# Self-attention run batch by batch, its projections kept in SBUF and moved there by direct transfers, with the head of the kernel and the loops written out

## The chip, the cores and the metric

The kernel runs on one core of one Trainium2 chip. The metric is the device time of one execution in microseconds (us), lower being better. The core has a matrix engine (TensorE, PE in the rows), a vector engine (VectorE, DVE), an activation engine (ScalarE, ACT), a general engine (GpSimd, POOL) and a queue engine that issues most of the transfers (SyncE, SP). Each engine works through its own instructions in order and waits on semaphores for the others.

## The reference, cut to what matters

One decoder layer on 2 batches of 1024 tokens with 256 features: layer norm, causal self-attention with 16 heads of 16 features, an 8-step recurrent state update, a feed-forward block, cross-attention to 77 context tokens, and a block of decision trees. The change touches the first two only:

```
x = x + attn_block(_layernorm(x))            # in it a second norm, _ln(x, g_attn, b_attn), comes first:
xn = _ln(x, g_attn, b_attn)
qkv = (xn @ qkv_w + qkv_b).reshape(b, s, 3, H, HD)       # H = 16 heads of HD = 16
scores = jnp.einsum('bhqd,bhkd->bhqk', q, k) / np.sqrt(HD)
scores = jnp.where(causal[None, None], -jnp.inf, scores)
attn_w = jax.nn.softmax(scores, axis=-1)
attn = jnp.einsum('bhqk,bhkd->bhqd', attn_w, v)
attn = attn @ out_w + out_b
x = x + attn
```

## The kernel before, in words

Everything is held transposed: 128 partitions carry features, the free axis carries tokens. The 2048 tokens are four **chunks** of 512; chunks 0 and 1 are batch 0, chunks 2 and 3 are batch 1. The queries and keys make four projection **tiles** of 128 features for each chunk (two of queries, two of keys), so there are 16 tiles. A tile is a float32 product in two matmuls (`qk_projection`, L1623). The values are another 8 groups of projections (L1636).

Self-attention works on **quads**: four heads of one batch. There are 8 quads. For each quad two things are computed.

1. The **maxima**. 36 **units** (L1664) multiply 128 queries by 128 keys of four heads, each into one PSUM bank of a ring of three (banks 5 to 7), with a second, masking matmul (L1667) on the 8 diagonal ones. VectorE reduces each unit (`maximum`, L1208), then reduces the 8 partial maxima (`gather`, L1219); TensorE transposes the result (`turn`, L1684); VectorE negates it (`negate`, L1226), and a transfer writes it as two extra rows of the queries (`load_max`, L560).
2. The **scores**, in 12 steps (L1692), with keys in the partitions. Queries and keys are split in a high and a low part, stacked as 3 x 16 rows a head, so that a fast one-pass matmul gives nearly float32 precision. ScalarE takes the exponential (L878), GpSimd masks the diagonal blocks (L737), TensorE multiplies by the values with a column of ones for the sums (`weigh`, L1710), ScalarE copies the result out (`read_out`, L890).

TensorE's order is written by hand: during quad n it runs the scores and `weigh` of n, and between them the units of quads n+1 and n+2 (`ahead`, by a list `plan` that shares 36 units over the 12 steps). Before quad 0 it must run all 36 units of quad 0 and the first 8 of quad 1.

All re-arranging goes through DRAM. The high and low parts (`part_hi`, `part_lo`) of each tile are stored three times (`store_parts`, L467), 12 transfers of 256 KB a chunk, and loaded again for each quad: q1 and k1 for the units (`load_first`, L533, L538), q2 and k2 for the scores (`load_second`, L548, L552). Results are stored (L473) and loaded back (`pack`, L483, L491), the sums inverted on VectorE (L1236), stored and spread over partitions (`spread`, L499, L503). The quads go tile by tile: both batches of the first tile, then both of the second. The four tiles of batch 1 for each of its two chunks are projected beside the units of quad 0 (`qk_beside`). The engines run quads 2 to 5 in a hardware loop of two turns (`over_iterations`); the others are written out.

At the head, GpSimd presets k1, k2, q1, q2 and vq; two of its instructions at L693 write rows of ones. VectorE, ScalarE and TensorE do the norms of four chunks in a fixed skew of five stages (`skewed`), and the projections start after chunk 3.

## Time and profile before

| | us |
|---|---|
| median of 3 runs | 1054.2 (1047.81 to 1059.79) |
| the profiled execution, its own time | 1045.27 |
| its span, first to last instruction | 1043.5 |
| TensorE busy in the span | 917.5 (88%) |
| VectorE busy | 597.1 (57%) |
| ScalarE busy | 472.9 (45%) |
| GpSimd busy | 178.5 (17%) |
| mean granted TensorE clock | 0.915 of 2.4 GHz |

The profiled execution lies 8.9 us below the median of the three runs and just under the fastest of them. Shares of the whole span are means over stages with different limits, so they say little on a stage. The self-attention ends at about 382 us; the rest of the layer follows and is not changed.

### The profile page before, as it was taken

How to read it: one execution, taken by the hardware profiler on the slowest of the kernel's cores; microseconds unless marked ns; L12 is line 12 of the kernel's file. 1: busy time of each engine (PE TensorE's matmuls, PEld its weight loads, DVE VectorE, ACT ScalarE, POOL GpSimd, SP SyncE). 2: the span in 40 equal slices, each digit the busy share in tenths (PEclk: the TensorE clock that was granted, in tenths of full speed). 3: DMA queues.
4: the chain of work that ended last, by engine and by line, in shares of the span. 5: the costliest groups of instructions: out<-in, count | busy, mean ns of one | idle time of the engine just before them, and what ended most of it. 6: DMA issues, size and time to landing. Idle time of an engine off the chain costs nothing. (4 is left out here: it accounts for less than half of the span.)

```text
span 1043.5 us, 11787 instructions
## 1 busy us (share of the span) xinstructions
PE 917.5 (88%) x3897; PEld 557.2 (53%) x3912; DVE 597.1 (57%) x898; ACT 472.9 (45%) x681; POOL 178.5 (17%) x206
## 2 busy tenths in 40 slices
PE   5776689999999986999997899988887898899997
PEld 3553345554555433544444777754333666667775
DVE  4635767777777415377786664453434555546554
ACT  2311055565665662466654455524534323434332
POOL 7920012211122211000002340000015700000000
PEclk9797789999999997899998999996657999899999
DMA  3056534323443115100000000122745200000000
GB/s 124 9 201 171 216 101 112 101 61 95 104 112 101 37 60 192 48 0 1 0 1 7 12 1 1 36 56 43 139 98 131 79 1 20 1 1 21 1 21 20
DMA packets 27953, 66.15 MB, mean 63 GB/s; under 512 B 6048, under 2 KB 8992, under 8 KB 27520
## 3 DMA queue, kind: packets, MB, share of 16 engines
q1 hardware_dynamic: 24896, 62.00, 21.2%
q0 software_dynamic: 1472, 2.37, 1.1%
q10 hardware_dynamic: 1536, 1.14, 0.4%
q8 instruction: 29, 0.48, 0.2%
q14 instruction: 20, 0.16, 0.1%
HBM read 37.09 MB, written 19.14 MB: 54 GB/s over the span
## 5 line engine op out<-in xcount | busy, mean ns | idle before, releaser
L1208 DVE TENSOR_REDUCE part_max<-psum 128x4 f32<-128x512 f32 x288 | 186.0, 687 | 78.2 <-PE psum L1664 46.4
L878 ACT ACTIVATE prob<-psum 128x1024 f32<-128x1024 f32 (+1 forms) x192 | 145.4, 809 | 92.8 <-PE psum L1692 92.1
L1664 PE MATMUL psum<-k,q 128*128 128x512 f32 x288 | 121.8, 468 | 22.4 <-DMA k<-k 16.5
L1692 PE MATMUL psum<-q,k 128*128 128x512 f32 (+3 forms) x384 | 96.9, 358 | 11.0 <-ACTq L865 9.9
L1664 PEld LDWEIGHTS psum<-k,q 128*128 128x128 f32 x288 | 52.7, 196 | 85.9 <-DVE part_max L1208 55.4
L1061 ACT ACTIVATE silu<-psum,wt_bias 128x512 f32<-128x512 f32 x64 | 40.6, 686 | 116.5 <-PE psum L350 108.6
L737 POOL TENSOR_SCALAR_AFFINE_SELECT prob<-prob 128x256 f32<-128x256 f32 x128 | 52.1, 416 | 240.0 <-ACT prob L878 239.0
L1710 PE MATMUL psum<-prob,vq 128*32 128x512 f32 (+3 forms) x768 | 81.8, 498 | 2.4 <-POOL prob L737 1.6
L1692 PEld LDWEIGHTS psum<-q,k 128*128 128x128 f32 x384 | 66.2, 191 | 32.2 <-issue 11.2
L1540 DVE TENSOR_TENSOR masked_lo<-masked,masked_hi 128x1024 fp32r<-128x1024 f32 x32 | 41.2, 1288 | 40.7 <-ACT masked_hi L1068 40.7
L348 PE MATMUL psum<-masked_hi,wt_hi 128*128 128x512 f32 x128 | 56.3, 440 | 3.6 <-DVE masked_lo L1540 3.6
L348 PE MATMUL psum<-tree_hi,wt_hi 128*128 128x512 f32 x128 | 56.5, 442 | 1.6 <-ACT silu L1061 1.6
L1529 DVE TENSOR_SCALAR decide<-psum,wt_bias 128x512 bf16<-128x512 f32 x32 | 24.0, 751 | 56.9 <-PE psum L350 56.9
L1861 PE MATMUL psum<-act_u,early 128*128 128x512 f32 x128 | 55.8, 592 | 0.0
L1861 PE MATMUL psum<-nrm,early 128*128 128x512 f32 x128 | 55.6, 592 | 0.0
L349 PE MATMUL psum<-nrm_lo,wt_hi 128*128 128x512 f32 x128 | 53.2, 415 | 0.0
L350 PE MATMUL psum<-tree_hi,wt_lo 128*128 128x512 f32 x128 | 52.5, 410 | 0.0
L1611 PE MATMUL psum<-ident,rs 128*128 128x128 f32 x192 | 36.0, 354 | 16.8 <-DVE rs L1120 10.3
L1388 DVE TENSOR_REDUCE xrow_max<-psum 128x4 f32<-128x312 f32 x64 | 29.5, 480 | 36.6 <-PE psum L1807 36.3
L350 PE MATMUL psum<-masked_hi,wt_lo 128*128 128x512 f32 x128 | 50.1, 392 | 0.0
L349 PE MATMUL psum<-masked_lo,wt_hi 128*128 128x512 f32 x128 | 49.9, 390 | 0.0
L1611 PEld LDWEIGHTS psum<-ident,rs 128*128 128x128 f32 x192 | 33.7, 260 | 24.5 <-DVE rs L1120 15.0
(156 smaller groups left out, 1632.8 us busy)
## 6 DMA issues: line engine op xcount, KB each, us to landing
q<-q SPq DMA_DIRECT2D x8, 768.0 KB, 6.5
k<-k SPq DMA_DIRECT2D x16, 384.0 KB, 8.2
xq<-xq_b SPq DMA_DIRECT2D x36, 128.0 KB
q<-part_hi SPq DMA_DIRECT2D x16, 256.0 KB
k<-part_hi SPq DMA_DIRECT2D x16, 256.0 KB
o<-stage SPq DMA_DIRECT2D x8, 512.0 KB, 7.0
wt<-in_wt SPq DMA_DIRECT2D x8, 512.0 KB, 4.3
nrm<-in_xT SPq DMA_DIRECT2D x4, 512.0 KB, 5.8
```

The costliest lines, as they stand in the source:

```text
L348: pe.matmul(out, rounded(w_hi), rounded(x_hi), start=start, stop=False)
L349: pe.matmul(out, rounded(w_hi), rounded(x_lo), start=False, stop=False)
L350: return pe.matmul(out, rounded(w_lo), rounded(x_hi), start=False, stop=stop)
L737: pool.affine_select(out=blk, in_=blk, compare_op=ALU.is_ge, fill=0.0, base=0, pattern=[[0, 2], [1, P]], channel_multiplier=-1)\
L878: act.activation(A.prob[0:A.keys, s % 2, p, :, q0:CH], psum[0:A.keys, 2 * p:2 * p + 2, q0:CH], ACT.Exp, scale=SCALE)\
L1208: dve.tensor_reduce(part_max[:].rearrange("q (j p i) k -> q p j i k", j=2, p=2)[:, :, :, i, kt], heads, AX_X, ALU.max).then_inc(A.s1_free, 1)
L1540: dve.tensor_tensor(rounded(masked_lo[:, st.buf]), masked[:, st.buf], masked_hi[:, st.buf], ALU.subtract)\
L1611: mm = pe.matmul(bank((L.bank(c), 4)[i])[:, t * P:(t + 1) * P], rs[:, c % 2, i, t:t + 1].to_broadcast([P, P]), ident[:], start=True, stop= ...
L1664: mm = pe.matmul(heads, A.q1[:, qd, i * P:(i + 1) * P], A.k1[:, qd, :, k0:k0 + P], start=True, stop=not diag)
L1692: mm = pe.matmul(psum[0:A.keys, 2 * p + j, q0:CH], A.k2[:, qd, p, j, kt * P:kt * P + A.keys], A.q2[:, qd, p, c * CH + q0:(c + 1) * CH], st ...
L1710: mm = pe.matmul(psum[32 * h:32 * h + 32, 4, q0:CH], A.vq[:, qd, kt, h, :], A.prob[:, s % 2, h // 2, h % 2, q0:CH], start=first, stop=last)
L1861: mm = pe.matmul(bank(2 * c + m), wx01[:, k, m * P:(m + 1) * P], state(n)[:, k, cols_of(c)], start=False, stop=k == 1, skip_group_check=True)
```

## The change

- The products of the query and key projections stay in SBUF, in `nat_hi` (rounded) and `nat_lo`: ScalarE writes each tile twice (`qk_high`), and GpSimd subtracts (`qk_low`), where VectorE did it before. There are no DRAM copies q3, k3, o3.
- The units take `nat_hi` itself as queries, in its natural layout of 8 heads in 128 rows, against k1 that is zero outside the quad's 64 rows. q1 is gone. k1, q2 and k2 are filled by transfers inside SBUF: 4 for k1, 18 for q2 and k2 of a quad (6 of 32 rows and 12 of 16 rows), where 5 and 3 did it from DRAM. The results go from `stage` to their places by 5 such transfers in place of 1 store and 1 or 2 loads.
- The quads go batch by batch. Only batch 0's 8 tiles are projected at the head; the 8 tiles of batch 1 are projected inside quads 1 and 3, one in each of their score steps 4 to 7, each in a bank of the ring of three.
- The head is written out by hand in a new order: projections of chunk 0 begin while the norms of chunks 2 and 3 are still under way, and the units of quad 0 stand between the norms. The values are projected after that, between the last units of quad 0, and ScalarE copies them out; GpSimd adds the bias when it packs them for a quad (`copy_values`).
- GpSimd's presets start without waiting for the constants; the two instructions at L693 are replaced by two transfers; presets of q1 and sums are gone.
- All quads are written out; the hardware loop is gone. The shares of `plan` are rounded another way (steps 3 and 5 have 1 and 4 units in place of 2 and 3).
- The second norm has a scratch of its own, since the spread sums now lie in `wide`.

```diff
-            def store_qk(batch):
-                for c in by_batch[batch]:
-                    for m in range(4):
-                        sp.wait_ge(qk_free, 4 * c + m + 1 + 3)
-                        store_parts(sp, q3 if m < 2 else k3, part_hi, part_lo, m, c % 2, ...)
+            def load_k1(n, done, at):
+                b, m, qd = place(n)
+                if n >= 2:
+                    sp.wait_ge(mx_turned, n - 1)
+                for h in range(4):
+                    rows = slice(64 * qd + HD * h, 64 * qd + HD * h + HD)
+                    sp.dma_start(k1[rows, qd, h, at].bitcast(F32), nat_hi[rows, 2 + m, at]).then_inc(done, 16)
+            def load_q2k2(n):
+                b, m, qd = place(n)
+                if n >= 2:
+                    sp.wait_ge(st_ps, 2 * SSTEPS * (n - 1))
+                for r in range(3):
+                    for p in range(2):
+                        rows = slice(64 * qd + 32 * p, 64 * qd + 32 * p + 32)
+                        sp.dma_start(q2[32 * r:32 * r + 32, qd, p, :].bitcast(F32), ...)
+                        for j in range(2):
+                            sp.dma_start(k2[32 * r + HD * j:32 * r + HD * j + HD, qd, p, j, :].bitcast(F32), ...)
+            for n in range(XQUADS):
+                if n + 2 < XQUADS:
+                    load_k1(n + 2, k1_in[qd], whole)
+                if 2 <= n + 1 < XQUADS:
+                    load_q2k2(n + 1)
+                if n >= 1:
+                    pack_self(n - 1)
+                if n >= 2 and n % 2 == 0:
+                    spread_self(n // 2 - 1)
+                if n + 1 < XQUADS:
+                    load_neg_max(n + 1)
...
+        QK_TILES = [(c, t) for c in range(2) for t in (2, 0, 3, 1)] \
+            + [(c, t) for m in range(KT) for c in (2, 3) for t in (2 + m, m)]
+        def qk_tile_of(n, step):
+            return QK_TILES[8 + 2 * (n - 1) + step - 4] if n in (1, 3) and 4 <= step < 8 else None
...
+            def qk_low(c, t):
+                pool.wait_ge(qk_raw, qk_at(c, t) + 1)
+                pool.tensor_tensor(nat_lo[:, t, at].bitcast(F32R), nat_lo[:, t, at], nat_hi[:, t, at], ALU.subtract)
...
+            def qk_high(c, t):
+                act.wait_ge(qk_ps, qk_at(c, t) + 1)
+                act.activation(nat_hi[:, t, at].bitcast(F32R), qk_bank(c, t), ACT.Identity, bias=v_("bqk", t))
+                act.activation(nat_lo[:, t, at].bitcast(F32), qk_bank(c, t), ACT.Identity, bias=v_("bqk", t))
...
+            for n in range(XQUADS):
+                pe.wait_ge(q2k2_in[qd], 16 * 18 * (n // 2 + 1))
+                pe.wait_ge(neg_in[qd], 16 * (n // 2 + 1))
+                for s in range(SSTEPS):
+                    scores(n, s, 0)
+                    ahead(n, s, 0)
+                    scores(n, s, 1)
+                    ahead(n, s, 1)
+                    if qk_tile_of(n, s):
+                        qk_projection(*qk_tile_of(n, s))
+                    if s > 0:
+                        weigh(n, s - 1)
```

On TensorE at the head, before the change, all norms come first (mean L1590, variance L1598, spreading L1611), then 8 tiles of batch 0 (L1623), then all values (L1636), then the units:

```order
6 L1611 MATMUL psum<-ident,rs 128x128 x8
7 L1598 MATMUL psum<-mean_w,wide 128x1 x4
8 L1611 MATMUL psum<-ident,rs 128x128 x8
9 L1598 MATMUL psum<-mean_w,wide 128x1 x4
10 L1611 MATMUL psum<-ident,rs 128x128 x16
11 L1623 MATMUL psum<-nrm,w 128x512 x16
12 L1636 MATMUL psum<-w,nrm 128x256 x32
13 L1664 MATMUL psum<-k,q 128x512
```

After the change the same place on TensorE (spreading L1542, tiles L1558, variance L1529, mean L1521, units L1592):

```order
3 L1542 MATMUL psum<-ident,rs 128x128 x8
4 L1521 MATMUL psum<-wide,mean_w 128x512
5 L1542 MATMUL psum<-ident,rs 128x128 x8
6 L1558 MATMUL psum<-nrm,w 128x512 x4
7 L1529 MATMUL psum<-mean_w,wide 128x1 x4
8 L1558 MATMUL psum<-nrm,w 128x512 x2
9 L1521 MATMUL psum<-wide,mean_w 128x512
10 L1558 MATMUL psum<-nrm,w 128x512 x4
11 L1592 MATMUL psum<-k,nat_hi 128x512
12 L1595 MATMUL psum<-causal_b,ident_b 128x512
13 L1592 MATMUL psum<-k,nat_hi 128x512
14 L1558 MATMUL psum<-nrm,w 128x512 x2
```

The first tiles stand ahead of the norms of chunks 2 and 3, and the values (L1570, not in these rows) have moved behind the fifteenth unit and later.

On TensorE in quad 1, from the third score step of its second half on, before the change (scores L1692, weigh L1710):

```order
147 L1692 MATMUL psum<-q,k 128x512 x2
148 L1664 MATMUL psum<-k,q 128x512
149 L1692 MATMUL psum<-q,k 128x512 x2
150 L1664 MATMUL psum<-k,q 128x512
151 L1667 MATMUL psum<-causal_b,ident_b 128x512
152 L1710 MATMUL psum<-prob,vq 32x512 x4
153 L1664 MATMUL psum<-k,q 128x512 x2
```

After it, at the same place (scores L1614, weigh L1631):

```order
157 L1614 MATMUL psum<-q,k 128x512 x2
158 L1592 MATMUL psum<-k,nat_hi 128x512
159 L1614 MATMUL psum<-q,k 128x512 x2
160 L1592 MATMUL psum<-k,nat_hi 128x512
161 L1595 MATMUL psum<-causal_b,ident_b 128x512
162 L1558 MATMUL psum<-nrm,w 128x512 x2
163 L1631 MATMUL psum<-prob,vq 32x512 x4
164 L1592 MATMUL psum<-k,nat_hi 128x512 x2
```

A tile of two matmuls has come in ahead of `weigh`; four such places are in quad 1 and four in quad 3.

On SyncE, one turn of the steady order before the change, of quad 1 (L560 is the write of the maxima):

```order
51 L533 DMA q<-q 64x1x1024
52 L538 DMA k<-k 16x1024 x4
53 L548 DMA q<-q 96x2x1024
54 L552 DMA k<-k 48x2x1024 x2
55 L473 DMA o<-stage 128x1024
56 L483 DMA nrm<-o 64x1x1024
57 L560 DMA q<-neg_max 2x16x128
```

After it, the last part of the turn of quad 2 (k2 and q2 loads L486 and L482, sums L500, results L502, inverse sums L508 and L511, maxima L493):

```order
58 L482 DMA q<-nat_hi 32x1024
59 L486 DMA k<-nat_hi 16x1024 x2
60 L482 DMA q<-nat_lo 32x1024
61 L486 DMA k<-nat_hi 16x1024 x2
62 L500 DMA sums<-stage 64x1x64
63 L502 DMA nrm<-stage 16x1024 x4
64 L508 DMA r<-recip 128x64
65 L511 DMA wide<-r 128x1x1024
66 L493 DMA q<-neg_max 2x16x128
```

The write of the maxima, the last row of each, now stands behind 4 + 18 + 5 transfers of its turn, and 2 more in every second turn, in place of 10 to 12.

## Rows read from the trace of the kernel before

**Rows 1.** Windows of the first stage: us, busy of each engine, granted clock.
```profile
20.00:40.00 20.00, 13.83 (x66) 12.44 (x66) 14.81 (x26) 6.00 (x12) 19.74 (x4) 0.74 0.00 0
60.00:80.00 20.00, 11.59 (x54) 9.87 (x52) 5.66 (x16) 0.00 (x0) 1.16 (x2) 0.86 0.53 204
80.00:100.00 20.00, 11.86 (x33) 6.30 (x34) 9.45 (x16) 2.07 (x3) 0.00 (x0) 0.71 0.70 166
120.00:140.00 20.00, 9.98 (x31) 5.97 (x30) 7.92 (x13) 4.57 (x5) 1.08 (x3) 0.60 0.50 171
160.00:200.00 40.00, 38.59 (x239) 20.64 (x238) 29.12 (x47) 22.39 (x32) 9.27 (x23) 1.00 0.33 87
```

**Rows 2.** Timeline of TensorE at the head: start, duration, what, idle before.
```profile
21.70 2.66 PE L1611 MATMUL psum<-ident,rs 128*128 128x128 f32 x16
...
43.77 14.02 PE L1623 MATMUL psum<-nrm,w 128*128 128x512 f32 x32
57.62 13.98 PE L1636 MATMUL psum<-w,nrm 128*128 128x256 f32 x64
88.14 0.77 PE L1664 MATMUL psum<-k,q 128*128 128x512 f32 x1 [16.55 <-DMA k<-k]
...
118.86 0.39 PE L1684 MATMUL psum<-ident,row_max 128*32 128x128 f32 x1 [1.24 <-DVE row_max L1219]
...
133.88 1.19 PE L1692 MATMUL psum<-q,k 128*128 128x512 f32 x2 [9.92 <-ACTq L865]
```

**Rows 3.** Timeline of ScalarE at the head: the first bias, the first exponential.
```profile
26.50 1.38 ACT L848 ACTIVATE nrm<-nrm,vec 128x512 f32<-128x512 f32 x2
...
134.00 1.28 ACT L878 ACT_TABLE_LOAD   x1 [21.80 <-DMA k<-part_hi]
```

**Rows 4.** Timeline of TensorE in quad 6, one score step and the next.
```profile
342.34 0.63 PE L1692 MATMUL psum<-q,k 128*128 128x512 f32 x2
342.81 0.39 PE L1664 MATMUL psum<-k,q 128*128 128x512 f32 x1
343.03 0.63 PE L1692 MATMUL psum<-q,k 128*128 128x512 f32 x2
...
344.05 1.06 PE L1710 MATMUL psum<-prob,vq 128*32 128x512 f32 x8
...
345.62 0.62 PE L1692 MATMUL psum<-q,k 128*128 128x512 f32 x2
```

**Rows 5.** Timeline of ScalarE: the third step of quads 1, 2, 4 and 5.
```profile
173.66 1.08 ACT L878 ACTIVATE prob<-psum 128x512 f32<-128x512 f32 x2 [1.44 <-PE psum L1692]
...
205.49 1.08 ACT L878 ACTIVATE prob<-psum 128x512 f32<-128x512 f32 x2 [1.33 <-PE psum L1692]
...
268.95 1.08 ACT L878 ACTIVATE prob<-psum 128x512 f32<-128x512 f32 x2 [1.33 <-PE psum L1692]
...
301.98 1.08 ACT L878 ACTIVATE prob<-psum 128x512 f32<-128x512 f32 x2 [1.32 <-PE psum L1692]
```

**Rows 6.** Lines by source: duration min/median/max in ns, where they lie.
```profile
L467 SPq DMA_DIRECT2D q<-part_hi x16: 657/1196/1472, 48.9 to 115.6; - x16
L642 SPq DMA_DIRECT2D quot_b<-stage x32: 508/589/610, 713.2 to 802.4; - x32
L1208 DVE TENSOR_REDUCE part_max<-psum x288: 629/692/695, 89.5 to 350.5; 128x4 f32<-128x512 f32 x144
L766 POOL TENSOR_TENSOR res<-res,x x8: 1267/1634/1728, 549.4 to 594.5; 128x512 f32<-128x512 f32 x8
L1147 DVE TENSOR_TENSOR rs<-rs x4: 161/163/3264, 15.8 to 34.0; 128x4 f32<-128x4 f32 x4
L693 POOL TENSOR_SCALAR k<-k,ident x2: 10617/10624/10632, 28.3 to 39.1; 2x4096 fp32r<-2x4096 f32 x2
```

**Rows 7.** Timeline of SyncE and VectorE after the last quad.
```profile
382.49 0.33 SPq L473 DMA_DIRECT2D o<-stage  x1
385.18 0.58 SPq L483 DMA_DIRECT2D nrm<-o  x1
...
390.99 0.55 DVE L1236 RECIPROCAL recip<-sums 128x64 f32<-128x64 f32 x1 [12.61 <-DMA sums<-o]
...
400.00 1.23 DVE L1282 TENSOR_TENSOR nrm<-nrm,den 128x1024 f32<-128x1024 f32 x1 [6.66 <-DMA den<-r]
```

More of the change, by code:

```diff
@@ L43 @@
 SCALE = HD ** -0.5
-R2 = 3 * HD
+LEAD = 8
 LOW = -1e30
@@ new lines, in layer @@
+        self_units = [(kt, i) for i in range(SEQ // P) for kt in range(i + 1)]
+        SUNITS = len(self_units)
+        self_todo = [(1, u) for u in range(LEAD, SUNITS)] + [(2, u) for u in range(LEAD)]
+        self_plan = [[] for _ in self_steps]
+        for _at, _unit in enumerate(self_todo):
+            done = [CH - st[2] + 64 for st in self_steps]
+            step = next(i for i in range(SSTEPS) if (_at + 0.5) * sum(done) <= SUNITS * sum(done[:i + 1]))
+            self_plan[step].append(_unit)
@@ L712, in _ @@
             pool.tensor_copy(causal_b[:], caus_f[:])
[L713 to L732 removed]
+            pool.memset(vq[:], 1.0).then_inc(zeros_set, 1)
@@ new lines, in _, with read_out @@
+            first_bias(3)
+            for u in range(8):
+                keep_values(u)
+            def read_out(n, c):
+                b, m, qd = place(n)
+                act.wait_ge(pv_ps, 2 * n + c + 1)
+                if n >= 2 and c == 0:
+                    last = n - 2
+                    act.wait_ge(num_in[last // 4][qd], 16 * 4 * (last // 2 % 2 + 1))
+                    act.wait_ge(sum_in[qd], 16 * (n // 2))
+                act.activation(stage[:, qd, c * CH:(c + 1) * CH], bank(4), ACT.Copy).then_inc(o_done, 1)
@@ new lines, in turn, with scores @@
+            def turn(n):
+                pe.wait_ge(mx_row, n + 1)
+                pe.wait_ge(*slot_free(turn_slot[n]))
+                pe.transpose(bank(5 + turn_slot[n] % 3, P)[0:32], row_max[:], ident[:]).then_inc(mx_turned, 1)
+            def scores(n, s, p):
+                b, m, qd = place(n)
+                c, kt, q0, diag, first, last = self_steps[s]
+                g = n * SSTEPS + s
+                if g > 0:
+                    pe.wait_ge(prob_ready, 2 * g + p - 1)
+                for j in range(2):
+                    mm = pe.matmul(bank(2 * p + j)[:, q0:CH], k2[:, qd, p, j, kt * P:(kt + 1) * P],
+                                   q2[:, qd, p, c * CH + q0:(c + 1) * CH], start=True, stop=True)
+                mm.then_inc(st_ps, 1)
@@ new lines, in weigh @@
+            def weigh(n, s):
+                b, m, qd = place(n)
+                c, kt, q0, diag, first, last = self_steps[s]
+                g = n * SSTEPS + s
+                if s == 0:
+                    pe.wait_ge(vq_ready, n + 1)
+                if first:
+                    pe.wait_ge(o_done, 2 * n + c)
+                if diag:
+                    pe.wait_ge(prob_masked, 2 * (n * DIAGS + sum(st[3] for st in self_steps[:s + 1])))
+                pe.wait_ge(prob_ready, 2 * g + 2)
+                for h in range(4):
+                    mm = pe.matmul(psum[32 * h:32 * h + 32, 4, q0:CH], vq[:, qd, kt, h, :],
+                                   prob[:, s % 2, h // 2, h % 2, q0:CH], start=first, stop=last)
+                if last:
+                    mm.then_inc(pv_ps, 1)
@@ new lines, in ahead @@
+            def ahead(n, s, quarter):
+                for at, u in share(n, s, quarter):
+                    unit(at, u)
+                if turns_after(n, s, quarter):
+                    turn(n + 1)
+            mean(ln1)(0)
+            mean(ln1)(1)
+            variance(ln1)(0)
+            variance(ln1)(1)
+            spread_out(ln1)(0)
+            mean(ln1)(2)
+            spread_out(ln1)(1)
+            qk_projection(0, 2)
+            qk_projection(0, 0)
+            variance(ln1)(2)
@@ new lines, in _ @@
+            qk_projection(0, 3)
+            mean(ln1)(3)
+            qk_projection(0, 1)
+            qk_projection(1, 2)
+            unit(0, 0)
+            unit(0, 1)
+            qk_projection(1, 0)
+            spread_out(ln1)(2)
+            variance(ln1)(3)
+            for u in range(2, 6):
+                unit(0, u)
+            qk_projection(1, 3)
+            qk_projection(1, 1)
+            for u in range(6, SUNITS):
+                unit(0, u)
+                if u == 9:
+                    spread_out(ln1)(3)
+                if u % 3 == 2 and u // 3 in range(4, 12):
+                    values_of(u // 3 - 4)
```

821 lines of the change are left out of this document (333 added, 488 removed).

## The prediction

> **What bounds the kernel now.** I read the windows by stage first, then the timelines of the head, then one quad step by step. The self-attention has three parts with three limits.
>
> The *head*, until the first scores at 133.88 us [rows 2], is bound by SyncE's queue. TensorE does its 8 tiles and the values by 71.6 us and then stands idle 16.55 us for k1, does the units, and stands idle 9.92 us more ahead of the first scores; ScalarE's wait there ends with a store of a key tile, 21.80 us [rows 3]. The stores are 48 transfers of 256 KB at a median of 1.196 us [rows 6], 57 us of queue between 48.9 and 122 us. In the windows TensorE is busy about half of the time there, and its granted clock is 0.60 to 0.86 [rows 1].
>
> The *quads* are bound by TensorE: 38.59 us busy of 40, clock 1.00, VectorE 29, ScalarE 22 [rows 1]. A step in which all parts are whole lasts 3.28 us from scores to scores (342.34 to 345.62), and TensorE is fed through all of it: 0.22 us from unit to next scores (342.81 to 343.03), and 1.06 for weigh [rows 4]. A quad takes 31.8 us (173.66 to 205.49) [rows 5].
>
> The *end* is a chain of transfers: last result stored at 382.49, loads from 385.18, inverse at 390.99, product at 400.00 [rows 7].
>
> **The change, part by part.**
>
> *Head: the removed waits.* All stores and the DRAM loads go. What is late next is TensorE itself, since its hand-written list now holds everything. In the trace the first bias of chunk 0 begins at 26.50 [rows 3]; its spreading (21.70, 2.66 us) now stands right after the variance of chunk 1, about 2 us earlier. But the spreading of chunk 1 stands ahead of the first tile, so I put that tile at 27.5. From there to the transpose of the maxima TensorE has 8 tiles, 14.0 us, and the values, 14.0 us [rows 2]; 36 units and 8 masks at 0.22, 9.7 us [rows 4]; and the rest of the norms of chunks 2 and 3, for which I take 12 us, from 13.83 busy in the window from 20 to 40 us that holds nearly all of that work [rows 1]. That is 49.7 us. For waits in order (variance of chunk 2, the first units, VectorE's norm work between maxima) I add 7 us. The transpose is then at 84.2. Before, 15.0 us passed from the transpose (118.86) to the scores (133.88), because the queue was full [rows 2]; now a gather and a negation (under 1 us in all), an issue of 0.6 and a landing stand there, 5 us. Scores begin at 89 to 90; I take 89.5. VectorE is no later: 36 maxima at 0.69, 25 us [rows 6], and some 15 us of norms after about 36 us end near 76. So the head gives 133.9 - 89.5 = 44.4 us. Bounds: without the 7 us of waits and with a chain of 4 us it is 52; with a quarter of the 49.7 us at half the clock, as the windows of the old head have it, it is 44.4 - 12.4 = 32.
>
> SyncE in the new head: 12 transfers for k1, then 18 for q2 and k2, at 0.59 us each as small transfers inside SBUF take [rows 6]: 18 us between about 30 and 60 us, under TensorE's work. The 18 for quad 1 stand behind the wait for the maxima of quad 0, go out from 86 to 97 us, and are wanted at 121. GpSimd's 8 subtractions at 1.6 us [rows 6] are done well before the values. The two instructions at L693, 10.6 us each, go; they were hidden, except as follows.
>
> *A rule on the shared port.* One VectorE instruction, L1147, took 3264 ns in place of 163, at 34.00 us, and it lies within L693 on GpSimd [rows 6]. The Trainium skill ("SBUF — State Buffer", Who interferes with whom) says that a VectorE instruction with two SBUF inputs waits for a GpSimd instruction that reads SBUF. That rule speaks against the change, which gives GpSimd 16 subtractions and 8 sums with SBUF inputs; by it the three additions of chunks 2 and 3 at the head could each wait up to 1.6 us, 5 us, against 3.1 us that go with L693. It would move the sum by under 2 us, since VectorE is not last there, and the maxima read PSUM.
>
> *Tiles in the quads.* 8 tiles now stand in steps 4 to 7 of quads 1 and 3, where TensorE has no free time [rows 4]. Before, they lay at the head among the units, under VectorE and the queue. Each costs 1.75 us [rows 2]: 14 us. From below: part of a step is waiting on VectorE's banks, so 1.0 us each, 8 us. From above: a tile takes a bank of the ring of three until ScalarE has read it twice (2 x 0.69, by the 1.38 of a bias pair [rows 3]); the unit three places later waits for that, but a weigh, two units and two scores, some 2.0 us, stand between, so I take nothing for it, and 1.25 us each as an upper bound, 24 us in all. ScalarE has room: 1.94 + 1.38 us in a step that grows to about 5.
>
> *Transfers in a quad.* 28 issues in a turn, 30 in every second one, at 0.59 us: 17 us of 31.8. The maxima's rows come last in it, but their value is ready only about 27 us into the quad, so nothing waits, with 8 us to spare. The price is that of stage to quot_b in the cross-attention, the same form [rows 6].
>
> *Written-out loops, new shares.* The quad outside the loop lasted 31.83 us (1 to 2), the pair across the middle 31.8 each, and only quad 4 to 5 lasted 33.03 [rows 5], where VectorE waited for the sums to land. I take 1 us for that and nothing for the loop. The Trainium skill ("Runtime: NRT & Kernel Launch", Instruction fetch mechanics) says that a taken branch makes a fetch stall. By it, unrolling would gain something at each turn; the rows of quads inside and outside agree to 0.1 us, so the sum has nothing of it.
>
> *End.* One store and one load become one transfer: 385.18 - 382.49 = 2.7 us, and the sums no longer stand behind the result's load (0.6) [rows 7]. The last chunks' product comes 4 us earlier; bounds 0 and 6.5. The order by batch changes nothing here: batch 0 was ready ahead of the end before, too.
>
> *Sum.* Span 1043.5 - 44.4 + 14 - 1 - 4 = 1008.1; with the 1.8 us that lie around it 1009.9. The median of three runs is 8.9 us above the profiled execution, whose time agrees with the lowest run within 2.5. I take half of that distance: **1014 us**, 3.8% below the median before.
>
> **The rivals.**
>
> 1. *The head runs cold.* TensorE waits in small pieces between norms, tiles and units, the granted clock stays between 0.5 and 1, and scores begin at 102. For: the old head had 0.60 to 0.86 [rows 1]. Against: the clock was 1.00 wherever tiles followed each other (14.02 us for 8). Time 1014 + 12.4 = 1026. Chance 0.13.
>
> 2. *The ring costs more than the tile.* Each tile costs 3.0 us for the bank and for exponentials behind two more copies on ScalarE. 8 x 1.25 = 10: 1024. Chance 0.10.
>
> 3. *Better than that.* Tiles half hidden (-6) and a head nearer its bound (-4 to -8): 1000 to 1004. Chance 0.12.
>
> 4. *SyncE's queue becomes the bound of every quad, and the kernel is slower.* If each issue takes as long as the stores at the head did, the 18 loads and 5 results stand between the start of a quad and the write of the maxima. A turn is then 24 issues plus a landing of 2.4 us, and 26 plus about 8 in turns with the inverse sums. Over six turns: 150 p + 31 - 191 us of delay. At 1.2 us it is 20 us, 1034. The whole gain of 35.4 is gone at p = 1.3 us; at the 1.472 of the longest q store [rows 6] it is 61 us, 1014 + 61 = 1075. Against: those were 256 KB each, these are 64 or 128 KB and the same form took 0.508 to 0.610. Chance 0.05, all slower.
>
> 5. *The change does not shorten the head.* The chain by chunks orders TensorE so badly that scores start near 124, 10 us before the old start, which the tiles eat: 1048, no change. Chance 0.04.
>
> The forecast itself, 1003 to 1024, has 0.56.
>
> **How the numbers follow.** The range must leave out no more than 0.2. It takes in cases 1 and 2 and most of 3, and the mild form of 4 (1034): 996 to 1036. A change under 1% (10 us) is about what a measurement of this kernel can't tell from none, as its three runs span 12 us. Faster by over 1%, under 1044: cases 0 to 3, 0.91. Same: most of case 5, 0.04. Slower: case 4, 0.05.
>
> **What would show it.** First exponential near 90 us (134 before). 8 tiles at the head and four in each of quads 1 and 3; those quads 38 to 39 us from third step to third step, the others 31.8. No TensorE wait on q2, k2 or the maxima's rows ahead of a quad; issues on SyncE near 0.6 us. GpSimd's subtractions near 1.6 us. Last weigh near 350, product of chunk 2 some 14 us later in place of 19. From there on the timeline is the old one, shifted by 35 us. I am wrong if the head's units wait one by one, if a quad's start waits for a transfer, or if the steps with tiles last over 6 us.

## The result and the profile after

The changed kernel takes 1004.8 us (median of 4 runs, 1001.6 to 1007.0); the kernel before, run beside it, 1051.0 us. The ratio is 0.9589 with the interval 0.9553 to 0.9625: 4.1% faster, 46.2 us. The profiled execution after has 1004.79 us and a span of 1002.8, so the two profiled spans differ by 40.7 us.

Windows of the first stage, which answer to [rows 1]:

```profile
20.00:40.00 20.00, 18.38 (x70) 11.35 (x69) 11.73 (x22) 9.31 (x17) 10.27 (x7) 1.00 0.04 8
40.00:60.00 20.00, 14.74 (x69) 9.06 (x67) 14.52 (x26) 8.56 (x16) 7.96 (x6) 0.97 0.50 93
60.00:80.00 20.00, 19.66 (x77) 16.07 (x78) 13.26 (x22) 3.94 (x7) 0.00 (x0) 0.85 0.05 8
```

TensorE (the first number) is busy 18.4, 14.7 and 19.7 of 20 us where it had been half idle, at a granted clock of 1.00, 0.97 and 0.85. The last mean hides a cold stretch: TensorE waited 2.76 us for VectorE's maxima ahead of a unit at 60.34, and from 60 to 64 us the granted clock was 0.50; it was back at 1.00 by 68.

Timeline of TensorE at the head, which answers to [rows 2]: the first tile, the end of the maxima of quad 0, the first scores.

```profile
27.03 2.05 PE L1542 MATMUL psum<-ident,rs 128*128 128x128 f32 x16 [1.62 <-DVE rs L1116]
28.91 1.45 PE L1558 MATMUL psum<-nrm,w 128*128 128x512 f32 x3
...
83.38 0.27 PE L1604 MATMUL psum<-ident,row_max 128*32 128x128 f32 x1
...
84.42 0.47 PE L1592 MATMUL psum<-k,nat_hi 128*128 128x512 f32 x1 [0.53 <-DVE part_max L1134]
...
87.50 0.62 PE L1614 MATMUL psum<-q,k 128*128 128x512 f32 x2
```

The first scores come at 87.50 in place of 133.88. Timeline of ScalarE, which answers to [rows 3] and [rows 5]: the table load and first exponential, the third steps of quads 0 to 2.

```profile
83.73 1.28 ACT L853 ACT_TABLE_LOAD   x1
88.16 1.94 ACT L853 ACTIVATE prob<-psum 128x1024 f32<-128x1024 f32 x2 [3.15 <-PE psum L1614]
...
93.17 1.09 ACT L853 ACTIVATE prob<-psum 128x512 f32<-128x512 f32 x2 [1.22 <-PE psum L1614]
...
124.04 0.60 ACT L853 ACTIVATE prob<-psum 128x512 f32<-128x512 f32 x1 [1.20 <-PE psum L1614]
...
162.75 0.60 ACT L853 ACTIVATE prob<-psum 128x512 f32<-128x512 f32 x1 [1.20 <-PE psum L1614]
```

The first exponential was at 135.30 and is at 88.16: 47.1 us earlier. From third step to third step a plain quad takes 30.87 us (31.8 before), a quad with four tiles 38.71.

TensorE's timeline in the step with the transpose of the maxima (transpose, scores, next unit), in quad 2, first in the kernel before, then in the changed one:

```profile
223.90 0.27 PE L1684 MATMUL psum<-ident,row_max 128*32 128x128 f32 x1
223.93 0.94 PE L1692 MATMUL psum<-q,k 128*128 128x384 f32 x4
225.40 0.50 PE L1664 MATMUL psum<-k,q 128*128 128x512 f32 x1 [0.53 <-DVE neg_max L1226]
```

```profile
181.16 0.27 PE L1604 MATMUL psum<-ident,row_max 128*32 128x128 f32 x1
181.19 0.94 PE L1614 MATMUL psum<-q,k 128*128 128x384 f32 x4
181.97 0.47 PE L1592 MATMUL psum<-k,nat_hi 128*128 128x512 f32 x1
```

Before, the transpose went into bank 7, which the units use too, and the third unit of the quad whose maxima come next waited until VectorE had read and negated it (`pe.wait_ge(A.neg, n + 1)` in `unit`). After the change the transpose takes the next bank of the ring in turn, and that wait is gone: the unit behind the scores goes out 0.7 us sooner. In the rows the wait shows only as the 0.53 in brackets.

Timeline of SyncE and VectorE after the last quad, which answers to [rows 7]:

```profile
342.68 0.59 SPq L500 DMA_DIRECT2D sums<-stage  x1
343.31 2.40 SPq L502 DMA_DIRECT2D nrm<-stage  x4
345.76 0.58 SPq L508 DMA_DIRECT2D r<-recip  x1
347.75 0.66 SPq L511 DMA_DIRECT2D wide<-r  x1
...
344.69 0.55 DVE L1157 RECIPROCAL recip<-sums 128x64 f32<-128x64 f32 x1 [29.29 <-DMA sums<-stage]
...
354.63 1.23 DVE L1166 TENSOR_TENSOR nrm<-nrm,wide 128x1024 f32<-128x1024 f32 x1 [6.30 <-DMA wide<-r]
```

The last weigh starts at 341.56 (381.31 before), the product 13.1 us behind it (18.7 before).

**Where the 46 us are**, by marks in the two traces: first exponential -47.1; from there to the last weigh 253.4 us in place of 246.0, +7.4; to the product -5.6; to the first SiLU of the trees -0.5 (815.00 and 769.18), in all -45.8. Behind it nothing is changed, but the trees took 233.6 us in place of 228.5. Windows of that stretch, before and after:

```profile
815.00:1043.50 228.50, 206.56 (x851) 155.57 (x866) 120.40 (x121) 80.64 (x106) 16.00 (x9) 0.97 0.04 12
```

```profile
769.20:1002.70 233.50, 212.15 (x866) 159.59 (x866) 120.65 (x121) 80.56 (x106) 16.12 (x9) 0.95 0.04 12
```

This is the same work at a granted clock of 0.95 in place of 0.97. In the profiled runs below, whose trees are unchanged, the stretch took 226.9 to 233.8 us, so this is from run to run. The difference of the medians, 46.2, is close to the 45.8 of the marks ahead of it.

### The profile page after: what moved, and what is told of

Its sections match the earlier page's. It is cut to its first block and busy times, and to the rows that moved or that the text cites. A ratio compares the mean times of both kernels' runs of the same rounds, so it can differ in the third digit from the quotient of the medians.

```text
span 1002.8 us, 11132 instructions
## 1 busy us (share of the span) xinstructions
PE 909.9 (91%) x3912; PEld 554.0 (55%) x3912; DVE 577.7 (58%) x865; ACT 485.7 (48%) x705; POOL 181.7 (18%) x218
## 5 line engine op out<-in xcount | busy, mean ns | idle before, releaser
L1592 PE MATMUL psum<-k,nat_hi 128*128 128x512 f32 x288 | 118.9, 454 | 6.4 <-DVE part_max L1134 5.0
L1614 PE MATMUL psum<-q,k 128*128 128x512 f32 (+3 forms) x384 | 96.7, 354 | 1.4 <-ACT prob L853 1.4
L1592 PEld LDWEIGHTS psum<-k,nat_hi 128*128 128x128 f32 x288 | 51.6, 190 | 66.1 <-issue 52.9
L1631 PE MATMUL psum<-prob,vq 128*32 128x512 f32 (+3 forms) x768 | 81.8, 498 | 1.3 <-POOL prob L677 1.2
L1614 PEld LDWEIGHTS psum<-q,k 128*128 128x128 f32 x384 | 65.1, 189 | 22.5 <-ACT prob L853 11.6
L979 ACT ACTIVATE xprob<-psum 77x1024 f32<-77x1024 f32 x32 | 31.6, 1015 | 28.0 <-PE psum L1770 27.3
L1542 PE MATMUL psum<-ident,rs 128*128 128x128 f32 x192 | 32.6, 329 | 12.5 <-DVE rs L1083 10.4
```

Source lines behind the costliest of these rows:

```text
L1592: mm = pe.matmul(heads, rounded(nat_hi[:, m, i * P:(i + 1) * P]), k1[:, qd, :, kt * P:(kt + 1) * P], start=True, stop=i != kt)
L1614: mm = pe.matmul(bank(2 * p + j)[:, q0:CH], k2[:, qd, p, j, kt * P:(kt + 1) * P], q2[:, qd, p, c * CH + q0:(c + 1) * CH], start=True, stop ...
L1631: mm = pe.matmul(psum[32 * h:32 * h + 32, 4, q0:CH], vq[:, qd, kt, h, :], prob[:, s % 2, h // 2, h % 2, q0:CH], start=first, stop=last)
```

## The experiments

Runs of one kernel differ by 0.5 to 2% in all, mostly behind the attention. In the traces the same quad of the changed kernel repeats within 0.05 us, and the first exponential lay between 87.34 and 88.61 in six profiled runs with the head of the changed kernel, and at 94.24 in a seventh (experiment 10). So small terms are read from marks: the first exponential, the third step of each quad, the last weigh, the product of the third chunk. Times without a range are medians of 2 to 6 runs. Where a cut of an edit leaves lines out, it has `...`.

**1. No tiles in the quads.** `qk_tile_of` gives none, and the projections of batch 1 are left out: batch 1 uses those of batch 0.

```diff
-            return QK_TILES.index((c, t))
+            return QK_TILES.index((c % 2, t))
...
-            return QK_TILES[8 + 2 * (n - 1) + step - 4] if n in (1, 3) and 4 <= step < 8 else None
+            return None
```

> The changed kernel without the 8 projection tiles in quads 1 and 3: batch 1 reuses the projections of batch 0. It leaves out the projections of batch 1. Theory (a tile costs its TensorE time and a little of the ring): the quads with tiles fall from 38.7 to 30.9 us, 8 x 1.96 = 15.7 us less than the changed kernel, near 989 us. By my prediction's price of 1.75 it is 14 us. Rival (part of a tile lies in time in which TensorE waits anyway, and the two long quads are long for another reason): under 10 us, above 995.

Measured: 982.4 us, ratio 0.9409 [0.935, 0.9467]. The third steps of quads 1 to 4 lie at 124.50, 155.38, 186.26 and 217.12: 30.9 us from each to the next, in the quads that had tiles too. To the last of them (307.80 against 323.00, with a start 0.45 us later) 15.65 us are gone, 1.96 for a tile. The first reading holds: a tile costs its TensorE time, 1.75, and on average 0.2 more.

**2. The wait behind the transpose put back.**

```diff
+                if u == 2 and n >= 1:
+                    pe.wait_ge(mx_neg, n)
                 if at >= 3:
                     pe.wait_ge(*slot_free(at))
```

> The changed kernel with one wait of the old one put back: the third unit of the quad after next, behind the transpose of the maxima, waits until VectorE has negated that transpose, as the fixed bank made it do. Nothing is left out. Theory (the bank of the transpose in the ring is what made the plain quads shorter): the step with the transpose grows by 0.7 us, plain quads from 30.9 to 31.6, six or seven times, 4 to 5 us in all, near 1009. Rival (the new shares of units in the steps made them shorter): no change, 1005.

Measured: 1008.0 us. Plain quads go from 30.87 to 31.6 us (quad 2: 163.32 to 194.93), tiled ones from 38.71 to 39.38. From the third step of quad 0 to that of quad 7 it is 234.2 us in place of 229.8, 4.4 us for six transposes. So 0.73 of the 0.95 us by which plain quads became shorter is this wait.

**3. The kernel before with its loop written out.**

```diff
-            with eng.Fori(int(peel_first), ITS - 1) as it:
-                for qd in range(QUADS):
-                    body(it, qd, 2)
+            for it in range(int(peel_first), ITS - 1):
+                for qd in range(QUADS):
+                    body(it, qd, 2)
```

> The kernel before with its loop over the quads written out on every engine; nothing else is changed. Theory: the loops cost nothing, ratio 1.00 within 0.2%, quads at 31.8. Rival (each turn of a loop costs a stall in the fetch of instructions, and this is part of the 0.95 us by which the plain quads are shorter in the changed kernel): quads inside the loop near 31.0, 3 to 5 us less in all, ratio 0.996.

Measured: from third step to third step 31.80 to 31.82 us, no shorter than in the loop (31.70 to 31.82 without the long quad). But the one long quad, 33.03 (268.95 to 301.98 [rows 5]), is gone. VectorE and SyncE there, first in the kernel before, then with the loop written out:

```profile
274.56 0.68 SPq L483 DMA_DIRECT2D nrm<-o  x1
275.51 0.66 SPq L491 DMA_DIRECT2D sums<-o  x1
...
281.34 0.55 DVE L1236 RECIPROCAL recip<-sums 128x64 f32<-128x64 f32 x1 [1.93 <-DMA sums<-o]
```

```profile
273.89 0.58 SPq L483 DMA_DIRECT2D nrm<-o  x1
274.59 0.62 SPq L491 DMA_DIRECT2D sums<-o  x1
...
280.26 0.55 DVE L1236 RECIPROCAL recip<-sums 128x64 f32<-128x64 f32 x1
```

In the loop the sums were issued 6.56 us behind the quad's third step, written out 4.85 us (third step at 269.74), and landed in time: VectorE's 1.93 us of waiting went. The whole kernel did not gain: 1056.4 against 1048.2, ratio 1.011 [1.0057, 1.0163]. Up to the product at 399.85 (400.00) the profiled run, which is the shortest of the six, shows nothing of a loss, and at the first SiLU it is 1.4 us late. Why the timed runs are 8 us longer isn't shown; at least they speak against any gain from written-out loops as such.

**4. The kernel before with a third of the stores.** `q3` and `k3` hold one part; the loads read it three times.

```diff
             for r in range(3):
                 part = part_lo if r == r_lo else part_hi
+                if r != 0:
+                    sp.sem_inc(done, 16)
+                    continue
                 sp.dma_start(out3[:, r, :, at], part[:, half, m_of, :]).then_inc(done, 16)
...
```

> The kernel before with one store of three: of each projection tile only the first of three copies goes to DRAM, and all three parts of the loads read it. It leaves out the low parts of queries and keys, so the scores lack their correction. 16 of 48 stores are left, and 9 more loads stand in each quad. Theory (the old head is bound by the queue of the stores, 1.2 us each): first scores come 25 to 35 us earlier than 133.9, near 100 to 108, and the time falls by about as much; quads stay at 31.8. Rival (the old head is bound by TensorE's order of work, or its cold clock): under 10 us earlier.

Measured: the first exponential at 109.11 in place of 135.30, 26.2 us earlier, quads of 31.8. So over half of the 47.1 us that went from the head was the queue of stores; which part of the other 20.9 us is the loads through DRAM, batch 1's tiles or the order of the work, no run separates. The time is 1034.8, ratio 0.9878 [0.9817, 0.9938], a gain of half of the 26.2. In the profiled run three steps, in quads 2, 4 and 6, took 5.4 to 6.7 us back, 18.6 in all, so that the last weigh is only 9.9 us earlier. Each is of this form on VectorE:

```profile
193.93 0.55 DVE L1242 RECIPROCAL recip<-sums 128x64 f32<-128x64 f32 x1 [5.62 <-DMA sums<-o]
```

My edit had put 9 more loads ahead of the sums, and a wait of VectorE for them stops the maxima and then TensorE. This led to experiment 6.

**5. Half of the values' projection.**

```diff
-                    for k in range(KT):
+                    for k in range(1):
...
```

> The changed kernel with half of the values' projection: each of the 16 products takes one half of the contraction only, which is left out of the result. TensorE has 7 us less to do between the first tile and the transpose of the maxima. Theory (the new head is bound by TensorE's own list): the first exponential comes 5 to 7 us earlier than 88.2. Rival (it is bound by VectorE's maxima and norms, which would leave TensorE waiting in its place): under 2 us earlier.

Measured: first exponential at 83.35, 4.8 us earlier for 7.0 us less of TensorE work (4.0 to 5.3 by the spread of the other heads); quads unchanged; 993.9 us. So TensorE's list sets some two thirds of the 7 us. Behind that VectorE's maxima are last: they run without a break from 73.28 on and end at 78.20, and the transpose waits for their gather and begins at 78.71.

**6. Twice the transfers for the same bytes.** Each of the 18 transfers of a quad's queries and keys is cut in two by columns.

```diff
-                        sp.dma_start(q2[32 * r:32 * r + 32, qd, p, :].bitcast(F32),
-                                     (nat_lo if r == 2 else nat_hi)[rows, m, :]).then_inc(q2k2_in[qd], 16)
+                        for at in (slice(0, CH), slice(CH, SEQ)):
+                            sp.dma_start(q2[32 * r:32 * r + 32, qd, p, at].bitcast(F32),
+                                         (nat_lo if r == 2 else nat_hi)[rows, m, at]).then_inc(q2k2_in[qd], 16)
...
```

> The changed kernel with each of the 18 transfers of queries and keys cut in two, so that the queue of SyncE has 18 more issues in each quad for the same bytes. Nothing is left out. Theory (an issue costs 0.6 us whatever its size, and the slack of the queue is small at one place): the sums of a quad are issued 11 us later, land near 182 in place of 171, and the reciprocal that stands in VectorE's maxima at 173 waits some 9 us, in quads 2, 4 and 6; 20 to 27 us in all, near 1030, while the other quads stay at 30.9 and no quad's start waits. Rival (my rival 4, in which the start of each quad waits for the row of the maxima): 3 to 8 us in every quad, first in quads without a reciprocal too. Third (the queue has room): under 2 us.

Measured: 1031.0 us, ratio 0.9847 [0.9777, 0.9918], 26 us more than the changed kernel by the medians, and 23 without the longest of the four runs (1047.9). By the marks 31.9 us are added up to the last third step: quads 2, 4 and 6 grow by 10.2, 9.6 and 9.4 us, quads 1, 3 and 5 by nothing, and quad 0 by 2.6. Timeline of SyncE and VectorE in quad 2:

```profile
179.61 2.49 SPq L488 DMA_DIRECT2D k<-nat_hi  x4
182.15 0.63 SPq L502 DMA_DIRECT2D sums<-stage  x1
...
184.19 0.55 DVE L1159 RECIPROCAL recip<-sums 128x64 f32<-128x64 f32 x1 [8.26 <-DMA sums<-stage]
```

and of TensorE behind it:

```profile
185.44 0.77 PE L1594 MATMUL psum<-k,nat_hi 128*128 128x512 f32 x1 [7.45 <-DVE part_max L1136]
```

An issue costs the same 0.62 us for half of the bytes. The queue does become the bound, but not as rival 4 had it: no quad's scores waited at their start. The 2.6 us in quad 0 are an idle stretch of TensorE ahead of a unit at 113.59: the loads of k1 for quad 2, the last in that queue, went out from 109.34 to 111.76, and the last of them landed at 113.50. In the changed kernel the sums are issued at 168.99 and the reciprocal comes at 173.11; with the 2 us that such a transfer takes to land (182.15 to 184.19), the slack there is 2 us, some three issues. Of the three reciprocals amid maxima it has the least (in quads 4 and 6 the sums are issued 5.7 and 4.7 us ahead, here 4.1), and the prediction looked at another place.

**7. The end of the last quad through DRAM.**

```diff
+                if n == XQUADS - 1:
+                    sp.dma_start(o3.rearrange("h s d n -> (h s d) n"), stage[:, qd, :]).then_inc(o_st, 16)
+                    sp.wait_ge(o_st, 16)
...
+                    return
...
```

> The changed kernel, in which the result and the sums of the last quad alone go through DRAM as before: one store, a wait, a load of the result and then one of the sums. Nothing is left out. Theory (the end is shorter because one landing and the place behind the result's load are gone): from the last weigh to the product of the third chunk 18 to 19 us in place of 12.7, 5.5 to 6.5 us more. My prediction's price: 4 us more. Rival (it was the order by batch that shortened it): under 1 us.

Measured: last weigh at 341.63, product at 360.40, 18.8 us between them, where the changed kernel has 13.1 and the kernel before 18.7. The whole term is this, 5.7 us. The time is 1008.6 us.

**8. Tiles in short steps.**

```diff
-            return QK_TILES[8 + 2 * (n - 1) + step - 4] if n in (1, 3) and 4 <= step < 8 else None
+            return QK_TILES[8 + 2 * (n - 1) + (2, 3, 10, 11).index(step)] if n in (1, 3) and step in (2, 3, 10, 11) else None
```

> The changed kernel with the four tiles of quads 1 and 3 in steps 2, 3, 10 and 11 instead of 4 to 7. These steps have small scores, and TensorE is not full in them: from the scores of the fourth step to those of the fifth pass 1.70 us, in which its scores, one unit and one weigh take about 0.9. Theory: a tile fills part of that time and costs 1.0 to 1.4 us in place of 1.96, so 4.5 to 7.5 us less than the changed kernel, near 999. Rival (every step is a chain through ScalarE and the ring, and a tile in it adds its whole time and the wait for a bank): 38.7 us for a quad with tiles as before, 1005 or more.

Measured: the tiled quads take 37.76 and 37.78 us in place of 38.71 and 38.68, 1.72 us a tile. Neither reading holds: the short steps have no free TensorE time to give, and what went is only the 0.2 us a tile above its TensorE time. In quad 4 another 1.1 us was lost: ScalarE issues three loads there, and one took 1.93 us in place of 0.86. The median, 998.4, is 6.4 us lower, but the product in the profiled run is only 0.7 us earlier; the rest lies in unchanged work behind.

**9. One small VectorE instruction moved.**

```diff
             dve.wait_ge(c_in, 64)
-            dve.tensor_scalar(b1_scaled[:], vec[:, VEC["b1"][0]:VEC["b1"][0] + KT], 1 / (DT * DT), None, ALU.mult)\
-                .then_inc(b1_set, 1)
...
                 if u == 0:
                     negate(0)
+            dve.tensor_scalar(b1_scaled[:], vec[:, VEC["b1"][0]:VEC["b1"][0] + KT], 1 / (DT * DT), None, ALU.mult)\
+                .then_inc(b1_set, 1)
```

> The changed kernel with one small VectorE instruction, the scaling of b1 (128 x 2), moved from the start to behind the first maxima of quad 1. Nothing is left out. In the changed kernel it takes 1.77 us at 6.22 and ends with GpSimd's first memset of k (1.04 to 7.96), and the squares behind it end at 7.99; before it took 0.17, since that memset began at 7.47 only. Theory (this instruction waits for the memset, and the chain of the first norm behind it): the squares end near 7.0, and everything to the first exponential is 0.5 to 1.3 us earlier, near 87. Rival (it is the memset that slows every VectorE instruction, or the head hides it): the squares still end at 8.0, or the first exponential stays at 88.2.

Measured: VectorE's first squares now take 0.69 us from 6.36 on, beside the memset that runs until 7.96, so the instruction was what waited. The first exponential came at 87.48, but the first tile no earlier (29.33, 28.91 in the changed kernel), and 87.48 lies within the spread of the other heads. A gain of the head is not shown, and so the 998.8 us (2 runs) is no measure of it.

**10. The wait and the old shares together.** The wait as in experiment 2, and:

```diff
-            step = next(i for i in range(SSTEPS) if (_at + 0.5) * sum(done) <= SUNITS * sum(done[:i + 1]))
+            step = next(i for i in range(SSTEPS) if i == SSTEPS - 1 or _at * sum(done) < SUNITS * sum(done[:i + 1]))
```

> The changed kernel with the wait behind the transpose of the maxima put back and the units of a quad shared out to its steps as before (4 3 2 2 4 3 4 4 4 3 2 1 in place of 4 3 2 1 4 4 4 4 4 3 2 1). Nothing is left out. Theory (the wait is 0.73 us of a plain quad, as measured, and the shares are what is left of the 0.95): a plain quad takes 31.8 us, as in the kernel before. Rival (the rest comes from the queries in their natural layout or from the transfers): 31.6, as with the wait alone.

Measured: 1012.3 us, plain quads 31.61 us, tiled ones 39.19 (39.38 with the wait alone). The shares are not the other 0.2 us: the step in which they take 0.27 us more is made up by the next four. Some 0.13 of it lies in the second step of each quad, 2.84 us in the kernel before and 2.71 in the changed one and here; what makes it stays open. The head of this run was 6 us late, first exponential at 94.24. The rows of VectorE at its start say why, here beside GpSimd's memsets:

```profile
6.16 8.69 DVE L1098 TENSOR_SCALAR b_scaled<-vec 128x2 f32<-128x2 f32 x1 [6.16 <-DMA mean_w<-in_mean_w]
...
1.04 6.93 POOL L634 MEMSET k<- 128x8192 f32 x1
7.90 6.93 POOL L635 MEMSET k<- 128x8192 f32 x1
```

**11. Five edits together**, nothing left out: tiles as in 8, the instruction as in 9, ScalarE's three loads on SyncE, the last group of the values behind the transpose, and at the end:

```diff
+            for half, done in ((0, den_in[1]), (1, den_last)):
+                at = slice(half * CH, half * CH + CH)
+                sp.dma_start(den[:, i, at], r3[i, :, at].rearrange("h (u n) -> h u n", u=1).to_broadcast([HT, HD, CH]))\
+                    .then_inc(done, 16)
```

> The changed kernel with five edits, nothing left out: the tiles of quads 1 and 3 in steps 2, 3, 10 and 11 (measured 1.85 us less in the two quads); the scaling of b1 later (0.5 to 1.3 less); the last of the 8 groups of the values behind the transpose of the maxima, where TensorE waits some 2 us for the first scores (1.0 to 1.7 less); the three loads of weights of ScalarE's queue, 256.50 to 258.71, on SyncE behind the maxima of quad 7 (0.6 less, 1.1 more by what the run with tiles in short steps showed at this place); at the end the transfer of the inverse sums ahead of the last part of the result, and their spreading in two halves, so that the third chunk's product waits for one (1 to 2 less). In all 5 to 8 us less in the trace up to that product, near 998. Rival (each edit is covered by something else): under 2 us, 1003 to 1005.

Measured: 995.8 us; the product at 351.00, 3.6 us earlier than in the changed kernel. The end gained 3.5 us (9.6 from weigh to product in place of 13.1), ScalarE's loads 0.56 us, but the first exponential came at 90.28. TensorE's rows say why:

```profile
82.47 0.29 PE L1621 MATMUL psum<-ident,row_max 128*32 128x128 f32 x1 [0.86 <-DVE row_max L1156]
...
89.22 0.70 PE L1631 MATMUL psum<-q,k 128*128 128x512 f32 x2 [0.88 <-ACT wide L827]
```

The transpose waited for VectorE, so it came no earlier, and the scores waited for the copy of the values.

**12. The same with the values back.**

```diff
-                if u % 3 == 2 and u // 3 in range(4, 11):
+                if u % 3 == 2 and u // 3 in range(4, 12):
...
-            values_of(7)
```

> The kernel of the run before with the last group of the values back among the units of quad 0; the other four edits stay, nothing is left out. In that run the first exponential came at 90.28, 2.8 us later than with the scaling of b1 moved alone (87.48): the transpose of the maxima came no earlier (82.47 and 82.66), since VectorE's last maxima end there, and the first scores then waited for ScalarE's copy of the values out of the same banks. Theory: the first exponential is back near 87.5 and all behind it 2.8 us earlier, the third chunk's product near 348.2 in place of 351.0, some 6.4 us ahead of the changed kernel's 354.63. Rival (the last group costs its 1.75 us wherever it stands): the product near 351.

Measured: 995.3 us, ratio 0.948 [0.9432, 0.9527]. First exponential at 87.81, last weigh at 338.94, product at 348.42, 6.2 us earlier than in the changed kernel (354.63). The time is 9.5 us below that of the changed kernel, of which the marks carry 6.2 up to the product and 7.0 up to the first SiLU (762.14). The intervals of the two ratios do not overlap. It is the fastest version that leaves nothing out, if only by 0.5 us beside experiment 11, which is within the noise; its product is 2.6 us earlier.

## Why the prediction was right, and where its terms were off

The forecast of 1014 us was 9 us high; 1004.8 lies in the range. By the marks the prediction had -35.4, and -45.8 was measured up to the trees. That is 10.4 us, and the part for the distance of one profile to the median, from 1009.9 to 1014, adds 4 in the same direction: this time the profiled execution lay on the median. The trees took 5 us longer than before at their lower clock, which the forecast had not. So the total is nearer than its terms, by luck.

*Head, -44.4 predicted, -47.1 measured.* The mechanism is shown for over half of it by experiment 4: without two thirds of the stores the old head loses 26.2 us. The list of TensorE's work held: transpose at 83.38 (84.2 predicted), then 4.1 us to the scores (5). The first tile came at 28.91 and not at 27.5, and the work from there took 54.5 us and not 56.7, so two errors cancel in part. Rival 1, scores at 102, is refuted: they came at 87.50. Its cause did appear in small, in the stretch at 0.50 from 60 to 64 us. TensorE was not the only bound: experiments 5 and 11 show VectorE's last maxima at its heels.

*Tiles, +14 predicted, +15.7 measured.* The place and the TensorE price of 1.75 held. "I take nothing for it", for the bank in the ring, was the error of size: 0.2 us a tile on average, 0.8 a tiled quad, and experiment 8 takes it away by other steps. Most of it is one wait in each tiled quad, the only one of TensorE there of over 0.1 us, behind the first tile:

```profile
132.52 0.48 PE L1592 MATMUL psum<-k,nat_hi 128*128 128x512 f32 x1 [0.59 <-ACT nat_lo L800]
```

ScalarE, which works in order, copies the result of the last quad (130.62) ahead of the tile's two readings (131.12 and 131.69), and the unit that needs the tile's bank waits for the second. In quad 3 the same 0.59 us stand ahead of a unit at 202.11. The rival with 3.0 us a tile is refuted.

*Plain quads, 0 predicted, -0.95 each measured.* This is the step that failed: "the others 31.8". I read the transpose's move into the ring as bookkeeping and cost only the tile's bank. The trace of before had the price, 0.53 us of idle TensorE behind a transpose. Experiment 2 shows 0.73 of the 0.95; experiments 3 and 10 show that neither loop nor shares are the rest.

Step by step, the 7.4 us by which the stretch from the first exponential to the last weigh grew are about: +15.7 for the tiles, -4.4 for the wait behind six transposes, -1.3 for the long quad, +0.6 for ScalarE's loads in quad 4, -1.3 for the second steps, and -1.2 for the first step of quad 0. Before, that step took 3.47 us at a granted clock of 0.50, after TensorE's long idle time, and takes 2.27 at 1.00 now; in experiment 4 it takes 2.28, at 1.00 too. The last 0.7 is in terms of under 0.25 us each, among them the one that follows.

*GpSimd's masks, not predicted.* The prediction says that the order by batch changes nothing at the end. It moves one wait. VectorE's two products of batch 0 (1.2 us each) fell into quad 7 before (375.79) and fall into quad 6 now (313.07). Beside them a mask of GpSimd takes 1.59 us from 314.09 in place of its median of 0.41 (before, one took 1.34 from 377.30), and TensorE waits for it:

```profile
316.09 0.85 PE L1631 MATMUL psum<-prob,vq 128*32 128x384 f32 x8 [0.82 <-POOL prob L677]
```

It costs 0.75 us in quad 6 and cost 1.0 in quad 7, so it all but cancels here. From the first scores to the last weigh this and the two waits of 0.59 are the only ones of TensorE over 0.5 us in the changed kernel. No run moves the product to prove the cause.

*The long quad, -1 predicted, some -1.3 measured.* It was the wait for the sums, as said. Written-out loops alone remove it too (experiment 3), so it is no proof of the shorter way of the sums. The Trainium skill ("Runtime: NRT & Kernel Launch", Instruction fetch mechanics) ties the stall of a taken branch to a target outside the two pages at hand, a condition that the prediction leaves out. Whether the start of this loop was outside them no run here shows; a stall does not show in the quads, 31.8 in the loop and out of it. New in its place are 0.56 us in quad 4, where ScalarE issues three loads.

*End, -4 predicted, -5.6 measured.* The mechanism held (experiment 7); its size was near the upper bound given. The two terms that the prediction names, 2.7 and 0.6, make 3.3; the 4 has 0.7 without a source. From the first issue to the reciprocal it is 2.0 us (342.68 to 344.69), and through DRAM in experiment 7, with a store and two loads, it was 9.0 (342.75 to 351.79).

*SyncE's queue.* Issues took 0.59 us at the median, as taken (the longest 2.16). "Nothing waits, with 8 us to spare" was near enough true of the row of the maxima (in quad 2 the queue stood idle for 6.7 us ahead of it, from 175.88 to 182.63), but the sums ahead of the reciprocal have 2 us to spare. Rival 4 had the right resource and the wrong place.

*The rule on the shared port* was weighed at under 2 us for the additions of the head. The trace agrees that there is such a wait: of VectorE's squares of 0.69 us one took 1.76, from 32.36 to 34.1, beside a GpSimd subtraction from 32.18 to 33.57. Since VectorE was not last there, it cost nothing that shows. The row that the prediction starts from fits less well: by the profile L1147 ran from 34.00 to 37.26, and GpSimd's L693 beside it went on until 38.97. The prediction did not see the waits at the start (below).

## What to carry to other kernels

Look in the trace for the short waits of the engine that sets the pace, tenths of a us in each repetition, and ask of each whether the edit removes it by the way: here a fixed bank with its own wait was worth 0.73 us in each of six quads, 4.4 us in all, as much as the end of the attention was expected to give.

When transfers are replaced by more and smaller ones, count issues up to every consumer in the queue's order, not only to the last one. The costly one is where the waiting engine feeds another, here a reciprocal in the middle of the maxima.

A step with little work in it is not a step with free time: put one piece in it and measure, before moving all.

## What was unexpected of the hardware

A VectorE instruction of 128 x 2 elements, 0.17 us in the kernel before, took 1.57 to 1.79 us in seven profiled runs of versions of the changed kernel that have it in this place, ending each time within 0.05 us of the end of GpSimd's first memset of k, and 8.69 us in an eighth, in which it ended with the second memset, at 14.85. Here is one of the seven, the changed kernel itself:

```profile
6.22 1.77 DVE L1098 TENSOR_SCALAR b_scaled<-vec 128x2 f32<-128x2 f32 x1 [6.22 <-DMA mean_w<-in_mean_w]
...
1.04 6.92 POOL L634 MEMSET k<- 128x8192 f32 x1
7.90 6.95 POOL L635 MEMSET k<- 128x8192 f32 x1
```

The Trainium skill ("SBUF — State Buffer", Who interferes with whom) says that `tensor_scalar` can enter a mode that takes the port pair shared with GpSimd, and that the one who comes second is fully blocked. The eight rows agree, and the next squares in the same place, a `tensor_tensor`, run beside the memset in 0.69 us once the scaling is gone (experiment 9). The eighth row shows more, once in eight: between two memsets that follow each other the waiting instruction missed its turn and waited for the next one too. In that run the first exponential came 6 us later (94.24 against 88.16), for an instruction whose result is wanted only behind the attention. In the other seven no gain from moving it is shown (experiment 9).

An issue on SyncE costs about 0.6 us whether it moves 64 KB or half of it (experiment 6), and on ScalarE it stands between exponentials: the same load took 0.86 us in the changed kernel and 1.93 in experiment 8.
